# One fused two-layer kernel: causal maxima masked on the Vector engine instead of TensorE, their splitting moved to POOL, and the Vector engine's loop closed at another point

## The reference, cut to what matters

```python
q = einsum('btc,oc->bto', x, Wq).reshape(B, T, 16, 8)      # the same for k, v
att = einsum('bqhd,bkhd->bhqk', q, k) / sqrt(8)
mask[i, j] = (j > i) & (j >= i - 31)                       # every key behind the query
att = where(mask, -inf, att)
att = softmax(att, axis=-1)
out = einsum('bhqk,bkhd->bqhd', att, v) @ Wo.T
```

## Time and profile before

| | |
|---|---|
| median of three executions | 1853.49 us |
| the profiled execution | 1856.61 us, its span 1854.6 us |
| PE busy | 1527.7 us (82%) |
| DVE busy | 1219.1 us (66%), 3591 instructions |
| ACT busy | 859.3 us (46%) |
| POOL busy | 518.1 us (28%) |
| loop of 12 turns | about 88.2 us a turn, from 324 to 1295 us |
| granted TensorE clock, mean | 0.912 |

### The profile page before, as it was taken

The page is one execution under the profiler, slowest core; times in us unless marked ns, Lnnn a source line. Parts: engine busy times, 40 slices in busy tenths (PEclk is TensorE's granted clock), DMA queues, the critical chain, the costliest instruction groups (busy, mean ns, idle before and its releaser), DMA issues.

```text
span 1854.6 us, 33561 instructions
## 1 busy us (share of the span) xinstructions
PE 1527.7 (82%) x10072; PEld 921.9 (50%) x10072; DVE 1219.1 (66%) x3591; ACT 859.3 (46%) x1787; POOL 518.1 (28%) x498
## 2 busy tenths in 40 slices
PE   2889999899999999999989898999999811356774
PEld 2455656464655555555555464656554311335553
DVE  5577878686878686877777786868766368811110
ACT  1436464645555554546464646464653512423331
POOL 1322222131313131312222222213130020048886
PEclk7879999999999999999999999999998755578898
DMA  2031221303030303031211212120303000044443
GB/s 72 1 80 40 49 63 30 77 16 86 7 86 12 80 16 83 24 69 39 53 51 41 55 37 55 37 75 18 80 8 86 8 12 1 1 78 94 96 85 58
DMA packets 83239, 90.71 MB, mean 49 GB/s; under 512 B 19520, under 2 KB 73024, under 8 KB 78528
## 3 DMA queue, kind: packets, MB, share of 16 engines
q1 hardware_dynamic: 71872, 80.76, 17.6%
q0 software_dynamic: 11264, 8.92, 3.6%
HBM read 58.95 MB, written 29.92 MB: 48 GB/s over the span
## 4 chain that ended last, share of the span: by engine, by line
PE 50%; issue 16%; DVE 16%; POOL 8%; DMA 3%; ACT 3%; SPq 1%; DVEq 1%; POOLq 0%; ACTq 0%
PE fa L681 7%; PE ba L587 6%; PE bo L840 6%; PE fa L673 6%; PE ba L582 5%; PE ba L593 4%; POOL out L552 4%; PE fa L691 4%; PE facc L691 2%; DVE passed L1497 2%; POOL got L522 2%; DVE nm L1265 2%; DMA QT<-nmT 2%; SPq L341 1%; PE fa L633 1%
## 5 line engine op out<-in xcount | busy, mean ns | idle before, releaser
L1020 ACT ACTIVATE probs<-ba 128x512 f32<-128x512 f32 x640 | 350.0, 600 | 179.2 <-PE ba L593 177.0
L458 POOL TENSOR_TENSOR x<-x,gd 128x512 f32<-128x512 f32 x144 | 182.4, 1267 | 612.5 <-ACT gd L998 596.0
L582 PE MATMUL ba<-QT,KT 75*128 75x512 bf16 (+3 forms) x1024 | 236.4, 309 | 26.4 <-ACT probs L1020 13.7
L587 PE MATMUL ba<-KT,QT 72*128 72x512 bf16 (+3 forms) x1024 | 230.8, 306 | 7.3 <-DVE nm L1265 3.4
L840 PE MATMUL bo<-probs,vp 128*32 128x512 f32 (+3 forms) x2048 | 193.1, 467 | 27.0 <-DVE ao L1278 26.0
L1265 DVE TENSOR_REDUCE nm<-ba 128x1 f32<-128x512 f32 x256 | 174.9, 683 | 33.2 <-PE ba L593 33.1
L582 PEld LDWEIGHTS ba<-QT,KT 75*128 75x128 bf16 x1024 | 87.9, 101 | 184.8 <-ACT probs L1020 99.5
L681 PE MATMUL fa<-f_nT,w 128*128 128x512 f32 x320 | 170.5, 614 | 3.4 <-DVE hh L1257 3.1
L673 PE MATMUL fa<-f_nT,w 128*128 128x512 f32 x320 | 169.7, 612 | 0.0
L593 PE MATMUL ba<-mask_k,identb 128*128 128x256 bf16 (+1 forms) x640 | 164.8, 258 | 0.0
L593 PE MATMUL ba<-mask_q,identb 128*128 128x256 bf16 (+1 forms) x640 | 164.0, 256 | 0.0
(11 more groups left out here) (279 smaller groups left out, 2679.3 us busy)
## 6 DMA issues: line engine op xcount, KB each, us to landing
QT<-qk_parts SPq DMA_DIRECT2D x96, 192.0 KB
KT<-qk_parts SPq DMA_DIRECT2D x96, 192.0 KB
qk_parts<-qkp SPq DMA_DIRECT2D x32, 384.0 KB, 2.5
fc<-in_L_ffn_fc_weight SPq DMA_DIRECT2D x32, 256.0 KB
xin<-in_L_attn_x SPq DMA_DIRECT2D x16, 256.0 KB, 7.4
qk_parts<-qkp SPq DMA_DIRECT2D x16, 256.0 KB, 2.7
out<-x SPq DMA_DIRECT2D x16, 256.0 KB, 2.3
xn_rows<-row SPq DMA_DIRECT2D x16, 256.0 KB, 7.8
```

The costliest lines, as they stand in the source:

```text
L458: pool.tensor_tensor(x1[:], x1[:], gd[:, e % 2], ALU.add).then_inc(S["s_x1g"], 1)
L582: pe.matmul(bank[:, col:col + w], lhsT=KT[0:K_ROWS, head, blk * P:(blk + 1) * P], rhs=QT[0:K_ROWS, head, blk * P:], start=first_, stop=False)
L587: pe.matmul(bank[:, col:col + w], lhsT=QT[0:QK_ROWS, head, blk * P:(blk + 1) * P], rhs=KT[0:QK_ROWS, head, 0:w], start=first_, stop=False)
L1020: act.activation(probs[:, pair % 3, f_], ba[n % 3][:], ACT.Exp, scale=SCALE).then_inc(S["s_exp"], 1)
```

## The change

1. `scores(..., by_key=False)` ends with the products of Q and K; the 640 matmuls that added `mask_q` are gone. For `by_key=True` the instructions are the same as before (the mask of both diagonal blocks is one matmul in either kernel).
2. `mask_q` is now 128x512, zero except for its last 128 columns. `maxima` has `tensor_tensor_reduce` in place of `tensor_reduce`: it adds the mask to the bank, multiplies by -1, writes the result back into the bank, and keeps the minimum in `nm`. One instruction takes one block of rows, so a fill of 256+256, which was one reduction, is now two. Behind each wait stands a nop (`apart`).
3. `max_parts` is POOL's: the first half in front of the `add_gated` at e = 6, the second behind the last `add_gated` of the phase.
4. DVE's y phase is split in front of `f_l2`; all that stood between it and the old split is now in the `rest` part, so the branch back of the loop stands behind `f_bias(f, 1)`. The order of DVE's steps is not changed by it.

```diff
-        mask_q = sb("mask_q", [P, P], BF16)
+        mask_q = sb1("mask_q", [P, SEQ], BF16)
...
+            last_ = mask_q[:, SEQ - P:]
+            const(pool.affine_select(last_, last_, [[-1, P]], ALU.is_ge, MASKED, base=0, channel_multiplier=1))
...
+            def max_parts(b, half):
...
+                pool.wait_ge(S["s_red"], FILLS * b + (half + 1) * FILLS // 2)
+                apart(pool)
+                pool.tensor_copy(nmp[:, half, :, 0], nm[:, :, heads]).then_inc(S["s_mstep"], 1)
+                pool.wait_ge(S["s_mstep"], done + 1)
...
+                    if b is not None and e == 6:
+                        max_parts(b, 0)
...
+                if b is not None:
+                    max_parts(b, 1)
...
-                    pe.matmul(bank[:, col:col + w], lhsT=QT[0:QK_ROWS, head, blk * P:(blk + 1) * P],
-                              rhs=KT[0:QK_ROWS, head, 0:w], start=first_, stop=False)
+                    last = pe.matmul(bank[:, col:col + w], lhsT=QT[0:QK_ROWS, head, blk * P:(blk + 1) * P],
+                                     rhs=KT[0:QK_ROWS, head, 0:w], start=True, stop=True)
...
+                apart(dve)
+                def lowest(head, blk, col):
+                    w = (blk + 1) * P
+                    return dve.tensor_tensor_reduce(bank[:, col:col + w], bank[:, col:col + w], mask_q[:, SEQ - w:], -1.0, -MASKED, ALU.add, ALU.min,
+                                                    nm[:, blk, head:head + 1])
                 if f in (0, 2):
-                    last = dve.tensor_reduce(nm[:, 3, h:h + 1], bank[:], X, ALU.max, negate=True)
+                    last = lowest(h, 3, 0)
                 elif f in (1, 3):
-                    dve.tensor_reduce(nm[:, 2, h:h + 1], bank[:, 0:384], X, ALU.max, negate=True)
-                    last = dve.tensor_reduce(nm[:, 0, h:h + 1], bank[:, 384:512], X, ALU.max, negate=True)
+                    lowest(h, 2, 0)
+                    last = lowest(h, 0, 384)
                 else:
-                    last = dve.tensor_reduce(nm[:, 1, h:h + 2], bank[:].rearrange("p (h k) -> p h k", h=2), X, ALU.max, negate=True)
+                    lowest(h, 1, 0)
+                    last = lowest(h + 1, 1, 256)
...
-                        if 5 <= e < 9:
-                            max_parts(0, e - 5)
-                if b is not None:
-                    for step in range(4):
-                        max_parts(1, step)
...
-                if rest:
-                    fc.b = f
-                    if_b(norm, 1)
...
+                if not rest:
+                    if_r(r_norm)
+                    if_f(f_bias, 0)
+                    if_r(r_center)
+                    if_f(f_bias, 1)
                     return
+                fc.b = f
                 if_f(f_l2)
...
                 if_b(outputs, 1)
+                if_b(norm, 1)
```

More of the change, by code:

```diff
@@ L458, in add_gated @@
                 pool.tensor_tensor(x1[:], x1[:], gd[:, e % 2], ALU.add).then_inc(S["s_x1g"], 1)
+            def max_parts(b, half):
+                heads = slice(half * HEADS // 2, (half + 1) * HEADS // 2)
+                done = 6 * b + 3 * half
+                pool.wait_ge(S["s_red"], FILLS * b + (half + 1) * FILLS // 2)
+                apart(pool)
+                pool.tensor_copy(nmp[:, half, :, 0], nm[:, :, heads]).then_inc(S["s_mstep"], 1)
+                pool.wait_ge(S["s_mstep"], done + 1)
+                apart(pool)
+                pool.tensor_tensor(nmr[:, :, heads], nm[:, :, heads], nmp[:, half, :, 0], ALU.subtract).then_inc(S["s_mstep"], 1)
+                pool.wait_ge(S["s_mstep"], done + 2)
+                apart(pool)
+                pool.tensor_copy(nmp[:, half, :, 1], nmr[:, :, heads]).then_inc(S["s_mstep"], 1)
+                pool.wait_ge(S["s_mstep"], done + 3)
+                apart(pool)
+                pool.tensor_tensor(nmp[:, half, :, 2], nmr[:, :, heads], nmp[:, half, :, 1], ALU.subtract).then_inc(S["s_nmp"], 1)
             def x_phase(f, b, t, g):
                 for e in range(U0):
+                    if b is not None and e == 6:
+                        max_parts(b, 0)
                     if g is not None and e == 3:
@@ L578, in scores @@
             for head, blk, col in groups:
-                first_ = not diagonal
                 if by_key:
@@ L582, in scores @@
                     pe.matmul(bank[:, col:col + w], lhsT=KT[0:K_ROWS, head, blk * P:(blk + 1) * P],
-                              rhs=QT[0:K_ROWS, head, blk * P:], start=first_, stop=False)
+                              rhs=QT[0:K_ROWS, head, blk * P:], start=not diagonal, stop=False)
                     diagonal.append(col // P)
@@ L586, in scores @@
                     w = (blk + 1) * P
-                    pe.matmul(bank[:, col:col + w], lhsT=QT[0:QK_ROWS, head, blk * P:(blk + 1) * P],
-                              rhs=KT[0:QK_ROWS, head, 0:w], start=first_, stop=False)
-                    diagonal.append((col + w) // P - 1)
-            n_, step_ = len(diagonal), max(diagonal[-1] - diagonal[0], 1)
-            blocks = bank[:].rearrange("p (n k) -> p n k", k=P)[:, diagonal[0]:diagonal[-1] + 1:step_]
-            mask = mask_k if by_key else mask_q
-            last = pe.matmul(blocks, lhsT=identb[:], rhs=mask[:, None, :].to_broadcast([P, n_, P]), start=False, stop=True)
+                    last = pe.matmul(bank[:, col:col + w], lhsT=QT[0:QK_ROWS, head, blk * P:(blk + 1) * P],
+                                     rhs=KT[0:QK_ROWS, head, 0:w], start=True, stop=True)
+            if by_key:
+                step_ = max(diagonal[-1] - diagonal[0], 1)
+                blocks = bank[:].rearrange("p (n k) -> p n k", k=P)[:, diagonal[0]:diagonal[-1] + 1:step_]
+                last = pe.matmul(blocks, lhsT=identb[:], rhs=mask_k[:, None, :].to_broadcast([P, len(diagonal), P]), start=False, stop=True)
             last.then_inc(S["s_st" if by_key else "s_S"], 1)
@@ L1429, in y_phase @@
                 if_b(outputs, 1)
+                if_b(norm, 1)
+                if_f(f_x1)
+                if_b(outputs, 2)
+                if_t(t_logits)
+                if_b(norm, 2)
+                if_f(f_logits)
+                if_f(f_gates)
+                if_f(f_rank)
+                if_b(outputs, 3)
             def y_whole(b, f, r, t):
```

30 lines of the change are left out of this document (1 added, 29 removed).

## The result

The changed kernel takes 1824.6 us (median of four executions, 1823.4 to 1825.1), the kernel before beside it 1855.1 us (1850.8 to 1858.3). The ratio is 0.984, 95% interval 0.981 to 0.986: **faster by 30 us**, 1.6%, where 1864.5 us and a slower kernel were forecast.

A forecast was written before the change was run, and what follows sets the result against it. PE was taken to bound the x phase, with DVE becoming its bound after the change, and DVE's branch to cost 4.0 us a turn. Terms +18 + 5 - 12 = +11 us on 1853.5 gave 1864.5 us, range 1826 to 1888.

The forecast's parts named there:

- I take 4.4 us, somewhat under the shortest row: DVE's branch at its new place: the stall taken as 4.4 us, with ends of 2.9 and 6.4 us kept.
- The 1.5 us for the clock: PE in the y phase: 1.5 us a turn lost to a lower clock behind its wait for DVE.
- The first rival: DVE's moved branch: the stall fits under the wait for sq, all 4.0 us a turn go, 1832 us; chance 0.29.
- The term was -12: The moved branch: 2.9 us a turn instead of 4.0, 11 x -1.1 = -12 us.
- The masks were forecast at +23 us: Masks in DVE's maximum pass: +18 us over 15 x phases with experts and +5 us in the last.
- POOL's splitting: End of the x phase: POOL's four steps take 1.1 us, hidden as long as they stay under 2 us.
- the 0.075 us for the accumulator: DVE's maximum pass: each masked reduction costs 0.075 us more than a plain one.
- The 5 us of the last x phase: The last x phase, without experts and already bound by DVE: masked reductions add 5 us.
- TensorE's 3.7 us: PE in an x phase: the removed query-major mask matmuls held it for 3.7 us, about 3.4 up to fill 37.
- 0.6 us was added for waits: x phase up to fill 37: 0.6 us of waits on DVE's 38.1 us, giving 38.7 us.
- The masked 512 at 0.67 to 0.68: Sign of being right: DVE's masked reductions of 512 columns start 0.67 to 0.68 us apart.
- DVE resuming near 951.3: Sign of being right: DVE stalls in front of the squared norms and resumes near 951.3 in the turn shown.

The follow-up runs named there:

- all_but_split: The changed kernel with DVE's branch back at its old place, masks and POOL's splitting kept; 1883.4 us, ratio 1.012 to the kernel before.
- masks_pool_quiet: all_but_split with SP holding back the loads of QT and KT until DVE's reciprocal is done; 1824.6 us, ratio 0.982.
- split_only: The kernel before with only the split of DVE's y phase, the branch back in front of the squared norms; 1817.8 us, ratio 0.977.
- split_and_pool: The kernel before with the branch moved and the maxima split by POOL, masks still on TensorE; 1808.5 us, ratio 0.973.
- no_query_masks: split_and_pool without any mask in the query-major pass, part of the computation left out; 1789.1 us, ratio 0.962.
- stall_uncovered: split_and_pool with the branch one step further on, behind f_l2, where DVE waits for nobody; 1859.7 us, ratio 1.001.
- the kernels of the second table: The kernel before, the changed kernel and variants of them, whose DMA records were read around the 11 branches back; the sequencer stands 2.76 to 7.71 us.

## Why the prediction was wrong

**The step that failed is "I take 4.4 us, somewhat under the shortest row".** The analysis before it was right in the main: the stall costs 4.0 us a turn (the split alone gave 3.71), it goes with the branch, some 3 us are covered at the new place (2.7 in the changed kernel: the last bias starts at 925.83, `sq` ends 2.7 us later), and the DMA share is 0.82 at one place and 0.03 at the other. The 1.5 us for the clock are right too: in the kernel before the granted clock is 0.50 for 3.4 us behind nine of the eleven waits for `ao`, in turns of 87.96 to 89.05 us, and stays at 1.00 behind the two shortest (1.48 and 1.60 us), in turns of 86.18 and 86.30. It even said that the stall is shorter where DMA is quiet if it is fetched over DMA. But then it took a value just below the shortest row, and every row it had was measured under load (a DMA share of 0.78 to 0.80 in all 11). Measured from the start of the last instruction, as there, the quiet stall is 1196.11 - 1193.10 = 3.0 us at the old place and 955.57 - 952.6 = 3.0 with f_l2 ahead. In front of the squared norms it is 2.0: the sequencer goes on at 927.70, and an instruction starts 0.12 us behind such a row elsewhere, so DVE was free to go on near 927.8 (an estimate), 2.0 us after 925.83. Two things make it so short. The fetch meets no load, and the sequencer runs ahead of the engine here: it takes the branch at 924.85, 1.0 us before the last bias starts, where at the old place it took it 0.08 us after the start of the copy (966.37 and 966.29). That second part was not in the prediction at all; it counted the stall from the last instruction at both places. It matters: with the body of all_but_split and DMA quiet (masks_pool_quiet) the stall from the start of the copy is 4.1 to 4.4 us, as long as the 4.4 that were taken. The first rival's condition held (a squared-norms row no later than before), and its 44 us are 42 in split_only. The term was -12, and is about -42.

**The masks were forecast at +23 us and measured less.** Against split_only the changed kernel loses 0.5 us a turn, 7 us of span, and 12 us by the ratios (0.984 and 0.977). POOL's splitting, which the prediction counted at nothing, gave 9 of it back; against split_and_pool the masks cost 0.96 us a turn and 17 us of span. The term that was too large is the 0.075 us for the accumulator: 0.01 to 0.05 measured. Rows 4, two reductions one behind the other, showed the dear case, and on another operation. The 5 us of the last x phase can't be told: behind the x2 of the last x phase with experts (1343.27 and 1329.92) 479.1 us remain in the changed kernel and 475.6 in split_and_pool, but 476.7 in the kernel before and 479.2 in split_only, which have the same masks, so 3.5 us are within what that stretch differs by anyway.

**TensorE's 3.7 us** are what the starts of rows 2 add up to; taking the matmuls away bought 1.39 us a turn (no_query_masks). They were used as if either engine's sum bounded the phase. 0.6 us was added for waits; in fact DVE is idle 1.9 us in the window. The x phase came out near the forecast (38.17 us beside 38.7) with both its parts off: DVE's load smaller, the waits larger.

**What was said to show it.** The masked 512 at 0.67 to 0.68: no, 0.61 to 0.65. An x phase of 38 to 39.5: yes. DVE hardly idle in it: no, 1.9 us; PE waiting for `nm`: yes, in its weight loads. "Issue" in front of the squared norms, DVE resuming near 951.3, and PE's wait grown to 2.3 us: no, a row released by ACT's `sq`, named there as the mark of the first rival. The wait for `ao` gone: yes. A new wait for b_rs or nmp: none; POOL's four steps took 1.33 us where 1.1 was counted, under the 2 us that were free.

**The cause of the stall.** It goes where the branch goes, and the sequencer stands 2.8 us or more each time. The prediction argued that by the 108 ns that the Trainium skill, "Advanced Engine Details and Errata", Control Flow Timing, gives for a compare-and-branch the stall would not belong to the branch. The row of the instruction itself is 63 ns, so the stall is not its own time, but it lies right behind it wherever the branch is put. The Trainium skill, "Runtime: NRT & Kernel Launch", Instruction fetch mechanics, has the target of a taken branch that is not in the fetched window brought by DMA before execution goes on. The trace agrees: an instruction packet lies in every one of these stalls, it starts later when the DMA engines are loaded (1.0 us after the branch or 2.6 to 3.9), and the sequencer goes on behind it. The prediction wrote that no row shows the fetch itself; the DMA records do. They don't name the engine or the instructions that a packet is for, so that it holds the target is inferred from its time.

**The range.** With 0.29 on a rival whose time was 1832, the lower end of 1826 left 6 us for the spread of that case. Its term for the branch was near (-44, and -42 in split_only); the masks and POOL's splitting together, +23 there and about +12 measured, put the time below the range.

## What to carry to other kernels

A loop's branch back can cost microseconds on its engine; here it did on DVE and on no other. Look at it in the timeline as "issue" behind the last instruction of the body, and where it is hidden in the rows of the loop's source line (COMPARE_BRANCH, and the sequencer's next row). Put it in front of a wait that is at least as long, and keep large transfers out of the same moment: a single wait on the DMA queue was worth as much here as rotating the loop. When a cost was seen only under load, the value for a quiet place is a case of its own, to be set against what covers it, and not the lowest row less a little. And count it from the branch itself, which the sequencer may reach before the engine's last instruction starts. And between two engines that hand over banks one by one, neither's sum is the bound; try the move in steps (8, 16, 32 fills) before moving all.

## What the runs showed of the hardware

- Behind DVE's taken branch back the sequencer stands 2.8 to 3.8 us with the DMA engines otherwise idle (DVE idle for 2.3 to 3.7 of them where nothing covers them), 3.6 to 3.7 at a DMA share of 0.44 to 0.45, and 4.8 to 7.7 at 0.76 to 0.81. One or two instruction packets of 8 KB lie in each of these stalls, and in the kernels of the second table execution goes on 1.3 to 1.8 us after the last has landed. Moving the loop's code by 32 or 64 instructions changes nothing in it.
- The branches back of PE, ACT, POOL and SP in the kernel before are followed by their next row within 0.27 us.
- A TensorE idle for 3.26 us is followed by a clock granted at 0.62 over 4 us (stall_uncovered); with waits of 0.95 us it stays at 1.00 through the loop of the changed kernel.
- DVE's masked reduction with an accumulator holds DVE 0.61 us for 512 columns behind a plain instruction and 0.65 behind another of its kind; the plain one 0.60.
- Mask matmuls of TensorE that a sum of starts puts at 3.7 us an x phase were worth 1.4 us when removed.
